# W3 and Wp multiplied into one matrix, W1a's bias moved into the last pass's ReLU, and W1a's products copied out by ScalarE

## The reference

```python
# L2, the attention block: 8 heads of 16, 8 heads of 16, then 1 head of 64
h = elu(gat_conv(x, ei, W1, as1, ad1, b1, 8, 16))
h = elu(gat_conv(h, ei, W2, as2, ad2, b2, 8, 16))
h = gat_conv(h, ei, W3, as3, ad3, b3, 1, 64)
h = h @ Wp + bp
return h / maximum(norm(h), 1e-12)
# gat_conv: h = x @ W; e = leaky_relu(<h, a_src>[src] + <h, a_dst>[dst]);
#           out = softmax of e over the edges of a node, times h[src], summed, + b
# L3, per edge, then summed by receiver
h = relu(concat(x[sender], edge_attr) @ W1a + b1a)
h = relu(h @ W1b + b1b)
```

## Time and profile before

| | us |
|---|---|
| median of 3 runs | 15976.06 (15976.02 to 15996.48) |
| the profiled execution, its own time | 15981.7 |
| span of its trace | 15980.0 |
| POOL busy in the span | 11257.5 (70%) |
| PE busy | 8190.7 (51%) |
| DVE busy | 6692.7 (42%) |
| ACT busy | 5666.0 (35%) |

### The profile page before, as it was taken

One profiled execution on the slowest core, in us unless ns is written; L12 is line 12 of the kernel. 1 busy time (PEld: TensorE's weight loads), 2 busy tenths in 40 slices (PEclk: granted clock), 3 DMA queues, 4 the chain that ended last, 5 costly groups with the idle time before them and its releaser, 6 DMA issues. The chain is left out here.

```text
span 15980.0 us, 259817 instructions
## 1 busy us (share of the span) xinstructions
PE 8190.7 (51%) x75456; PEld 7411.3 (46%) x75456; DVE 6692.7 (42%) x24144; ACT 5666.0 (35%) x13371; POOL 11257.5 (70%) x11862
## 2 busy tenths in 40 slices
PE   6555552565664763434432444432344444888886
PEld 4555441455554653333332333332344443777775
DVE  5555554777775863333335333335222224211112
ACT  2555551677774531222221222221111112333332
POOL 4777767677775457777767777776777775577776
PEclk9776765878877975666665666665555555799998
DMA  4444442222223743444432444443333332344443
GB/s 153 162 161 162 162 142 57 96 93 91 92 93 120 257 155 93 146 146 146 146 117 72 146 146 146 146 143 60 77 85 85 85 85 54 119 146 146 146 146 97
DMA packets 895395, 1965.03 MB, mean 123 GB/s; under 512 B 392230, under 2 KB 471026, under 8 KB 854067
## 3 DMA queue, kind: packets, MB, share of 16 engines
q0 software_dynamic: 361120, 582.27, 15.9%
q1 hardware_dynamic: 426179, 797.11, 14.6%
q10 hardware_dynamic: 107776, 582.40, 9.5%
HBM read 1095.74 MB, written 894.54 MB: 125 GB/s over the span
## 5 line engine op out<-in xcount | busy, mean ns | idle before, releaser
L112 POOL DMA_INDIRECT eg_got<-gat_table,eg_rows x4992 | 4714.7, 944 | 1542.1 <-issue 1512.5
L112 POOL DMA_INDIRECT e_got<-table,e_rows x3328 | 3155.6, 948 | 1031.2 <-issue 1004.6
L1321 PE MATMUL eg_ps_sum<-eg_got,eg_equal 128*128 128x136 f32 (+1 forms) x9984 | 2070.8, 382 | 280.3 <-DVE eg_got L1409 256.5
L1328 ACT ACTIVATE eg_outs<-eg_ps_sum 128x544 f32<-128x544 f32 (+1 forms) x1248 | 675.1, 541 | 4279.2 <-PE eg_ps_sum L1321 4268.9
L1321 PEld LDWEIGHTS eg_ps_sum<-eg_got,eg_equal 128*128 128x128 f32 x9984 | 1965.5, 291 | 344.2 <-ACT eg_outs L1328 189.1
L117 POOL DMA_INDIRECT sorted_rows<-sort_rows,sort_dest x1664 | 1615.9, 971 | 532.8 <-issue 495.9
L1353 PE MATMUL eg_small<-ident,eg_score 128*128 128x128 f32 (+1 forms) x312 | 138.6, 444 | 3176.1 <-DVE eg_score L1392 3176.1
L1353 PEld LDWEIGHTS eg_small<-ident,eg_score 128*128 128x128 f32 (+1 forms) x312 | 47.2, 151 | 3203.5 <-DVE eg_score L1392 3203.5
L1390 DVE TENSOR_TENSOR eg_diff<-eg_small,eg_got 128x128 f32<-128x128 f32 (+1 forms) x312 | 79.1, 253 | 2732.6 <-DMA eg_got<-gat_table,eg_rows 2732.6
L1621 DVE TENSOR_SCALAR e_got<-e_ps_second 128x512 f32<-128x512 f32 x416 | 287.6, 691 | 1758.0 <-PE e_ps_second L1604 1727.5
L567 PE MATMUL e_ps_sum<-e_got,e_equal 128*128 128x64 f32 x3328 | 628.8, 352 | 676.1 <-DMA e_got<-table,e_rows 676.1
(11 more groups left out here) (528 smaller groups left out, 20828.1 us busy)
## 6 DMA issues: line engine op xcount, KB each, us to landing
gat_out<-eg_outs ACTq DMA_DIRECT2D x208, 1152.0 KB
eg_equal_b<-equal_d SPq DMA_DIRECT2D x312, 512.0 KB
out<-e_outs ACTq DMA_DIRECT2D x208, 512.0 KB
out<-e_outs ACTq DMA_DIRECT2D x104, 1024.0 KB
values<-e_zeros_b SPq DMA_DIRECT2D x104, 768.0 KB
values_q<-e_zeros_b SPq DMA_DIRECT2D x104, 768.0 KB
sort_value<-values_q SPq DMA_DIRECT2D x104, 768.0 KB
e_value<-values SPq DMA_DIRECT2D x104, 768.0 KB
```

Source lines behind the costliest of these rows:

```text
L112: return e.indirect_dma_start(out, None, table, bass.IndirectOffsetOnAxis(ap=index, axis=0), **kw)
L1321: last_i = e.matmul(ps_sum[q % 2][:, i, 0:FG], equal[q % 4][:, i, :], got[k][:, t, :], start=True, stop=True)
L1328: e.activation(outs[k % 2][:, tiles, 0:FG], ps_sum[q % 2][:, :, 0:FG], ACT.Copy).then_inc(copied.sem, 1)
```

## The change

Three edits are made together.

1. `g2c` loads W3 transposed and Wp, multiplies them on PE, and appends the product to W3: the open layer's weight becomes [128, 64+64]. The scores are formed from the first 64 columns, straight from PSUM; the table holds the second 64 columns. So the third attention layer sums rows that have been multiplied by Wp already.
2. `g3c` has no `lin_p` any more. One product b3·Wp is added to bp once (`close.add_bias`), and that sum is the bias of `GatClose`. `in_steps` is gone: DVE does close, squares' sum, scaling and norm of one chunk and goes on to the next. ACT takes the products with W1a out of PSUM with a plain copy, interleaved by hand with its other work (`scalar_through`). SP loads the first two chunks of own rows ahead of the last pass's weights.
3. b1a is a column [128, 1] and becomes the bias operand of the ReLU in `e3`.

```diff
-            e.activation(h_t[q % 4][:, :, :], ps_first[q % 2][:, :, :], ACT.Relu).then_inc(relued.sem, 1)
+            e.activation(h_t[q % 4][:, :, :], ps_first[q % 2][:, :, :], ACT.Relu, bias=bias_a[:, :]).then_inc(relued.sem, 1)
...
# GatOpen
+            e.dma_start(self.w_t[:, :], ins[f"L2_gnn_W{n}"].rearrange("k o -> o k")).then_inc(self.after_in, 16)
+            e.dma_start(self.w_after[:, :], self.after).then_inc(self.after_in, 16)
...
+    def tensor(self, e):
+        e.wait_ge(self.w_in, 48)
+        if self.after is not None:
+            e.wait_ge(self.after_in, 32)
+            e.matmul(self.ps_w[:, 0:self.HF], self.w_t[:, :], self.w_after[:, :], start=True, stop=True).then_inc(self.joined, 1)
+            e.wait_ge(self.w_made, 1)
+
+    def join_weights(self, e):
+        e.wait_ge(self.joined, 1)
+        e.tensor_copy(self.w[:, self.kept_at:], self.ps_w[:, 0:self.HF]).then_inc(self.w_made, 1)
...
-            e.tensor_copy(hh, ps[:, :, :]).then_inc(out, 1)
+            e.tensor_copy(hid[:, :, 0:HF], ps[:, :, self.kept_at:]).then_inc(out, 1)
-            e.tensor_tensor(s_prod, hh, across(self.a_src[:, :], k), ALU.mult).then_inc(out, 1)
+            e.tensor_tensor(s_prod, h, across(self.a_src[:, :], k), ALU.mult).then_inc(out, 1)
...
# g3c, SP: the own rows of chunks 0 and 1 now ahead of the last pass's weights
+            close.sync_first(e)
...
-            close.sync(e)
             for j, ts in enumerate(CHUNKS):
+                if j + close.ring < n_chunks:
+                    close.sync_rows(e, j + close.ring)
                 lin_a.done(e, j)
...
# g3c, PE
-            in_steps(lambda j: None, lambda j: lin_p.tensor(e, j), lambda j: lin_a.tensor(e, j))
+            e.matmul(ps_bias[:, 0:D], bias_3[:, 0:1].to_broadcast([D, P]), w_p[:, :], start=True, stop=True).then_inc(bias_made, 1)
+            for j in range(n_chunks):
+                lin_a.tensor(e, j)
...
# g3c, DVE
-            in_steps(joined, normed, projected)
+            e.wait_ge(bias_made, 1)
+            close.add_bias(e, ps_bias[:, 0:D])
+            for j, ts in enumerate(CHUNKS):
                 close.vector(e, j)
                 e.sem_inc(closed, 1)
...
# g3c, ACT
+            for j in range(n_chunks + 1):
+                if j < n_chunks:
+                    close.merge.scalar(e)
+                if j:
+                    if j >= 3:
+                        e.wait_ge(hid_out[(j - 1) % 2], (j - 1) // 2 * 16)
+                    lin_a.scalar_through(e, j - 1, project, slice(0, 3))
+                if j < n_chunks:
+                    e.wait_ge(closed, j + 1)
+                    e.activation(sq[:, :, :], y[:, CHUNKS[j], :], ACT.Square).then_inc(squared, 1)
+                if j:
+                    lin_a.scalar_through(e, j - 1, project, slice(3, 4))
+                if j < n_chunks:
+                    e.wait_ge(measured, j + 1)
+                    e.activation(root[:, :], length[:, :], ACT.Sqrt).then_inc(rooted, 1)
+                if j:
+                    lin_a.scalar_through(e, j - 1, project, slice(4, None))
+                if j < n_chunks:
+                    norm.scalar(e, j)
...
+    def scalar_through(self, e, j, evacuate, some=slice(0, None)):
+        def out(b, ts):
+            e.wait_ge(self.made, b + 1)
+            n = ts.stop - ts.start
+            evacuate(e, b, ts, n, self.ps_o[b % self.n_o][:, 0:n, :])
+        todo = list(self.batches(j))
+        for i in list(range(len(todo) + 1))[some]:
+            if i < len(todo):
+                self.scalar(e, j, slice(i, i + 1))
+            if i:
+                out(*todo[i - 1])
```

More of the change, by code:

```diff
@@ L2235, in gat_layer, with gat_next @@
         return out
-    def gat_next(self, n, heads, ch, tables, out, next_heads, next_ch):
+    def gat_next(self, n, heads, ch, tables, out, next_heads, next_ch, after=None):
+        ins = self.ins
         HF = heads * ch
@@ L2241, in gat_next @@
         ph = Phase(self.nc, f"g{n}c")
-        close = GatClose(self, ph, n, heads, ch, *tables, out, ring=1)
+        close = GatClose(self, ph, heads, ch, *tables, out, ins[f"L2_gnn_b{n}"], ring=1)
         elu = Elu(ph)
@@ L2269, in vector @@
             close.collect.vector(e)
+            if after is not None:
+                opened.join_weights(e)
             for j in range(n_chunks + 1):
@@ L2292, in block23 @@
         tables = self.gat_tables
-        for n, heads, ch in ((1, HEADS, CH), (2, 1, D)):
+        for n, heads, ch, after in ((1, HEADS, CH, None), (2, 1, D, ins["L2_gnn_Wp"])):
             out_g = self.gat_layer(n, HEADS, CH, *tables)
-            tables = self.gat_next(n, HEADS, CH, tables, out_g, heads, ch)
+            tables = self.gat_next(n, HEADS, CH, tables, out_g, heads, ch, after)
         rows_g, own = tables
@@ L2312, in block23 @@
         ph = Phase(self.nc, "g3c")
-        close = GatClose(self, ph, 3, 1, D, rows_g, own, out_g)
+        close = GatClose(self, ph, 1, D, rows_g, own, out_g, ins["L2_gnn_bp"])
         norm = LayerNormChunk(self, ph)
-        w_p, bias_p = ph.sb("w_p", [D, D]), ph.sb("bias_p", [P, D])
-        w_a, bias_a = ph.sb("w_a", [D, H]), ph.sb("bias_a", [P, H])
+        w_p, bias_3 = ph.sb("w_p", [D, D]), ph.sb("bias_3", [D, 1])
+        ps_bias = ph.ps("ps_bias", [P, BANK])
+        w_a = ph.sb("w_a", [D, H])
         sq = ph.sb("sq", [P, CHUNK, D])
@@ L2416, in normed, with project @@
                 norm.vector(e, j)
[L2418 to L2421, removed]
-            in_steps(joined, normed, projected)
-        def scalar(e):
[L2425 to L2432, removed]
+        def scalar(e):
+            def project(e, b, ts, n, ps):
+                j = ts.start // CHUNK
+                at = slice(ts.start - CHUNKS[j].start, ts.stop - CHUNKS[j].start)
+                e.activation(hid[j % 2][:, at, :], ps, ACT.Copy).then_inc(lin_a.out, 1)
+            for j in range(n_chunks + 1):
[17 more added lines that the diff above has]
+                    norm.scalar(e, j)
@@ L2433, in block23 @@
         ph.run(sync=sync, gpsimd=close.collect.gpsimd, tensor=tensor, vector=vector, scalar=scalar)
         out, last = self.dram("out3", (EP, H)), self.dram("last3", (2, T, H))
-        self.attr_pass("e3", table, out, last, (w_attr, w_mid, b_rows, one_rows), (w_own, w_right, w_left, w_c_t, w_join, bias_e))
+        self.attr_pass("e3", table, out, last, (w_attr, bias_a, w_mid, b_rows, one_rows), (w_own, w_right, w_left, w_c_t, w_join, bias_e))
         self.finish_sums("f3", 0, out, last, H)
@@ L2752, with __init__ @@
 class GatClose:
-    def __init__(self, kn, ph, n, heads, ch, table, own, out, ring=2):
+    def __init__(self, kn, ph, heads, ch, table, own, out, bias_row, ring=2):
         self.kn, self.heads, self.ch, self.HF, self.table, self.own, self.ring = kn, heads, ch, heads * ch, table, own, ring
         HF, FG, FO = self.HF, self.HF + heads, self.HF + 2 * heads
-        self.bias_row = kn.ins[f"L2_gnn_b{n}"]
+        self.bias_row = bias_row
         self.agg = ph.sb("agg", [P, NT, FO])
@@ L2777, in sync_rows, with sync_first, add_bias @@
         e.dma_start(self.hid[j % self.ring][:, :, :], nodes(self.table)[:, CHUNKS[j], :]).then_inc(self.own_rows[j % self.ring], 16)
-    def sync(self, e):
+    def sync_first(self, e):
         self.sync_small(e)
-        for j in range(len(CHUNKS)):
+        for j in range(self.ring):
             self.sync_rows(e, j)
+    def add_bias(self, e, more):
+        e.wait_ge(self.small_in, 32)
+        e.tensor_tensor(self.bias[:, :], self.bias[:, :], more, ALU.add).then_inc(self.ve, 1)
+        e.wait_ge(self.ve, self.c(1))
     def vector(self, e, j):
```

55 lines of the change are left out of this document (25 added, 30 removed).

## The result

The kernel after takes **15902.4 us** (median of 4 runs, 15902.38 to 15903.52); the kernel before, run beside it, 15976.6 (15976.02 to 15996.48). The ratio is 0.9951, with a 95% interval of 0.994 to 0.9963: 74.1 us less. The forecast was 15898.7 and the range 15884 to 15920.

What follows compares the result with a forecast made beforehand. Phases add, each with its own bound: DVE's chain in `g3c`, POOL's gathers in the last pass. -78.9 + 0 + 1.0 + 0.5 + 0 = -77.4 us, from the median 15976.1 to 15898.7; range 15884 to 15920.

Steps and rivals of the forecast that it cites:

- The main term: `g3c`, first close to last product: DVE's chain falls from 245.5 to 166.6 us, 78.9 us less.
- The root's load in the open: `g3c`, chunks 1 to 6: ScalarE's table load follows batch 2's product copy, so the root comes 1.46 us late.
- the load hides after all: Rival in `g3c`: the root's table load is hidden, 8.8 us less, 15890; chance 0.12.
- The drain rival: `g3c`: a table switch costs a drain too, each root 1.4 us later, 8.3 us more, 15907; chance 0.12.
- The gathers: `g3c`: 21 us a chunk, hidden behind DVE's 22.4; rival that they pace it at 24: 15909, chance 0.06.
- The start of `g3c`: Weights landing some 5 us later use up DVE's 5.17 us of idle time: 0, bounds -1.4 and +4.
- `g2c`: Chunk 0's start 1 us later, bounds 0 and 6; the wider W3 product 0.5 us, bounds 0 and 3.6.
- The ReLU's bias: Last pass, 416 ReLUs: up to 0.124 us each, 52 us of ACT time, 0 on the path.
- slower: Last pass: PE's clock stays at 1.2 GHz, 1080 us more for the whole pass, about 16980; chance 0.03.
- three small terms: `g3c` start 0, `g2c` start 1.0 and the wider W3 product 0.5 us, added to the -78.9.
- the forecast's case: Whole kernel: the forecast holds, 15893 to 15904 us by its own bounds; chance 0.63.

Runs made afterwards that it cites:

- e2: Changed kernel with DVE again taking W1a's products out of PSUM after the next chunk's norm, ScalarE in its old order; 15931.6 us.
- e1: Changed kernel with ScalarE taking the root ahead of batch 3's turned tiles and the copy of batch 2's products; 15887.0 us, ratio 0.9947 to the kernel before.
- e7: Changed kernel with DVE waiting for all 98 gathers before chunk 0 of `g3c`; 16004.7 us.
- e5: Changed kernel with DVE's wait for the product W3·Wp put ahead of its clearing in `g2c`; 15905.2 us.
- e4: Changed kernel with the last pass's ReLU without its bias operand, b1a left out of the computation; 15893.2 us.
- e3: Changed kernel with ScalarE copying all turned tiles and products of a chunk in one block behind the norm's root, not interleaved; 15934.7 us.
- e6: Changed kernel with the transposed load of W1c issued behind the four loads of `w_attr` on SP; 15898.6 us.
- e8: Changed kernel with the edits of e1 and e6 together; 15888.2 us, ratio 0.9944 to the kernel before.

## Why the prediction was right, point by point

**The main term.** -78.9 was forecast, -78.0 measured. It is right in both halves: what leaves DVE (e2: the 35.8 us of waits come back with the adds) and what ACT then sets. The root's load in the open was forecast at 1.46 us a chunk and a wait of some 1.7; the trace has 1.62, and e1 gives 7.7 us back when the load is hidden. So the rival "the load hides after all" did not happen in this order, but its price of 8.8 us was near: e1 is that case.

**What was mis-sized.** The stretch came out at 167.5 us, not 166.6. Chunk 0 took 21.44 instead of 20.97, the next four 22.67 instead of 22.43; the last two (22.30) and the tail (10.8 for 11.0) were a little shorter. The working took its durations from the earlier trace rows, a chunk at 13552, after POOL's gathers had ended; the shorter phase runs mostly beside them. e7 shows the price: with no gathers beside it chunk 0 takes 20.95, and what grows is three one-input operations. The Trainium skill ("SBUF — State Buffer", Who interferes with whom) has it that DVE shares a pair of ports with GpSimd, that one-input operations between SBUF tensors can hold the pair whole, and that `tensor_reduce` never does and `tensor_tensor` only against reads. The trace agrees in kind: of DVE's small operations only TENSOR_SCALARs grew, and the slow gathers are those that start inside an operation with two inputs (e7). The three other TENSOR_SCALAR lines of the phase (L2406, L2640, L2823) stay at 174 to 175 ns, and their place explains it: one has no gather beside it, and the others start 0.14 to 0.45 or 0.84 to 0.85 us after a gather's start, while the grown ones start at 0.64 to 0.74. So the trace doesn't show the pair held for the whole of a gather.

**The drain rival.** Between the load's end at 13442.38 and the root lie 0.02 us, and the wait is 1.62, not the 3.1 that the rival would give. By the Trainium skill ("ScalarE: Activation LUTs", What ACT_TABLE_LOAD costs) a drain would stand there; this trace, like the earlier trace rows, shows none.

**The gathers.** Forecast at up to 21 us a chunk beside a denser DVE; they took (113.9 + 29.6) / 98 = 1.46 us each, 20.5 a chunk. DVE waited for none in chunks 1 to 6, not at 21.39 us a chunk either (e1), where the gathers need 20.7 and the margin is 0.7 us.

**The start of `g3c`.** 0 was right, for the reason given: the later weights used up the slack. It was a narrow thing, since the hold behind the transposed load grew to 8.57 us (7.0 to 8.6 in the seven profiles with this order).

**`g2c`.** 1 us was forecast for the start and 0.5 for the wider product. The first is 0.05: the load of W3 was wholly under the clears. Without that cover, put at 12, chunk 0 starts 9.3 later (e5). The second can't be told: `g2c` to `fg3` is 1.7 us longer in this profile, within the 5 us over which it scatters.

**The ReLU's bias.** 90 ns, inside the bounds 0 and 124, and hidden (e4). The part of "slower" that rested on PE's clock in `e3` didn't occur: the granted clock stayed 0.90. What it would have cost wasn't tried.

**From -77.4 to 74.1.** The profiles differ by 79.3 us, 3.8 of it upstream of the change; the medians differ by 74.1. The profiled execution of the kernel before lay 5.6 above its median (15981.7 against 15976.1), and the forecast carried that offset over. After there is none (profiled 15902.42, median 15902.44). So the profiled time after was forecast at 15904.3 and came out at 15902.4, 1.9 lower, and the median was forecast 3.7 too low: the offset explains the sign, and no part of the change does. How near the number came is partly luck, since the misses are smaller than the scatter. The stretches that the change touches gave 76.2 us in the profiles (-78.0 + 1.7 + 0.1) where 77.4 were forecast; the 3.8 us of scatter ahead of them carried the profiled time below its forecast; and the runs of the kernel before lie up to 20 us apart. One inner sum of the prediction is also off: the bounds of its three small terms (-1.4 to +4, 0 to 6 and 0 to 3.6) give 15896 to 15911 for the forecast's case, not 15893 to 15904. The stated range doesn't hang on it.

## What to carry to other kernels

When work moves to an engine that switches tables, write out that engine's order for one chunk with times: the copies gain only if they stand in its gaps (e3 gains nothing over e2), and a load needed for a short operation should be issued in the shadow of the engine that produces its input, here by placing the root ahead of a copy that waits for PE. When a phase shrinks, take the durations for the forecast from a chunk that runs beside the same background work as all of them will. Put a transposed load of single numbers last on its queue, or check what stands behind it.

## What the runs showed of the hardware

- DVE and POOL slow each other although they wait for nothing of each other: a gather's POOL time is 997 ns in the mean with DVE idle and 1162 beside it, and three 128x14 operations of DVE go from 175 to 228, 275 and 283 ns (e7). It is a matter of place: a gather that starts inside a 128x896 operation with two inputs takes up to 1.88 us, and a TENSOR_SCALAR that starts 0.64 to 0.74 us into a gather lasts almost to its end; the others keep their time.
- A transposed load of 8192 single numbers holds the next issue on its queue for 4.49 us when it comes ahead of the own rows (before), and for 7.0 to 8.6 us behind two chunks of them (seven profiles). Moved behind the other weights it leaves that same issue at 0.35 us (e6, e8).
- PE's granted clock in `g2c` is higher in the kernel after, whose product there is twice as wide. The windows of the kernel after show it (the third number from the right, 1.00 being the 2.4 GHz level); those of before have 0.50 in all three:

```profile
10868.00:11000.00 132.00, 21.32 (x94) 19.04 (x94) 79.68 (x113) 10.43 (x17) 102.18 (x82) 0.55 0.45 82
11000.00:11110.00 110.00, 26.89 (x118) 24.86 (x119) 71.49 (x110) 12.38 (x21) 88.98 (x70) 0.58 0.30 48
11110.00:11180.00 70.00, 15.91 (x86) 14.37 (x84) 34.51 (x67) 6.30 (x11) 40.19 (x38) 0.62 0.33 39
```

So the 1.2 GHz level held throughout before, and the higher one is granted for a part of the time after. DVE paces that phase, and no gain of time could be found. Why it rises is open.
